# Four-layer gated cross-attention: mixed attention moved to a third lane with one PSUM bank, one bank of scores in the top-k lane beside it, two weight packs in one reloaded buffer

## What is computed

```python
x = x + tanh(g_xattn[0]) * performer(layernorm(x), ctx)          # causal linear attention, 16 heads of 8
x = x + tanh(g_ffn[0])   * (attention(layernorm(x)) + top2_linear_experts(layernorm(x)))
x = x + tanh(g_xattn[1]) * topk64_attention(layernorm(x), ctx)   # 8 heads of 64
x = x + tanh(g_ffn[1])   * gated_experts(layernorm(x))
x = x + tanh(g_xattn[2]) * attention(layernorm(x), ctx)          # 16 heads of 8
x = x + tanh(g_ffn[2])   * gelu_experts(layernorm(x))            # 8 experts and a shared one, 128 to 512 to 128
x = x + tanh(g_xattn[3]) * topk32_attention(layernorm(x), ctx)   # 16 heads of 8
x = x + tanh(g_ffn[3])   * mixed_attention(layernorm(x))
```

## Time and profile before

| what | value |
|---|---|
| median of three runs (lowest, highest) | 2736.93 us (2734.93, 2739.3) |
| the profiled execution, its own time | 2744.56 us |
| its span, first to last instruction | 2742.8 us |
| PE, DVE, ACT, POOL busy share of the span | 86%, 75%, 51%, 33% |
| blocks that hold MixedAttention beside other work | 3 x ORDER_3_0, 3 x ORDER_1_0, ORDER_LAST |

### The profile page before, as it was taken

The page is one execution under the profiler, slowest core; times in us unless marked ns, Lnnn a source line. Parts: engine busy times, 40 slices in busy tenths (PEclk is TensorE's granted clock), DMA queues, the critical chain, the costliest instruction groups (busy, mean ns, idle before and its releaser), DMA issues. The chain is left out here.

```text
span 2742.8 us, 41506 instructions
## 1 busy us (share of the span) xinstructions
PE 2347.1 (86%) x12585; PEld 1739.3 (63%) x12585; DVE 2063.7 (75%) x8036; ACT 1388.9 (51%) x3333; POOL 915.8 (33%) x1398
## 2 busy tenths in 40 slices
PE   5888888999889788899989878889998898889876
PEld 3555675676576567576657656657765665766655
DVE  1498969867696796958779589695878859698692
ACT  2444565644535356664543546566362355656441
POOL 4141214246244122424525221332542512142432
PEclk9889889899999889988999889998999898899997
DMA  5000000000000000000000000000000000000000
GB/s 227 7 1 1 1 1 1 1 7 3 7 3 1 2 1 1 1 1 7 3 7 3 1 2 1 1 1 7 3 1 6 3 1 1 1 1 1 1 1 4
DMA packets 9069, 22.14 MB, mean 8 GB/s; under 512 B 642, under 2 KB 7810, under 8 KB 8066
## 3 DMA queue, kind: packets, MB, share of 16 engines
q1 hardware_dynamic: 8834, 19.33, 1.9%
HBM read 18.28 MB, written 1.05 MB: 7 GB/s over the span
## 5 line engine op out<-in xcount | busy, mean ns | idle before, releaser
L182 DVE MATCH_REPLACE8 workQ<-top_eight,workQ 128x256 f32<-128x256 f32 x1664 | 692.6, 439 | 0.0
L184 DVE MAX8 top_eight<-workQ 128x8 f32<-128x256 f32 x1664 | 641.6, 441 | 0.3
L218 POOL TENSOR_TENSOR att_pQ<-att_pQ,top_rest 128x512 f32<-128x512 f32 x192 | 244.2, 1272 | 333.6 <-ACT top_rest L211 333.4
L719 PE MATMUL bank<-workP 128*128 128x256 f32 x1024 | 297.4, 417 | 35.2 <-ACT att_pP L849 24.4
L719 PEld LDWEIGHTS bank<-workP 128*128 128x128 f32 x1024 | 188.3, 203 | 111.7 <-issue 61.5
L849 ACT ACTIVATE att_pP<-bank,att_nmaxP 128x256 f32<-128x256 f32 x512 | 215.2, 476 | 76.0 <-DVE att_nmaxP L898 75.1
L898 DVE TENSOR_REDUCE att_nmaxP<-bank 128x2 f32<-128x512 f32 x256 | 178.3, 708 | 94.6 <-PE bank L719 94.0
L234 ACT ACTIVATE att_pTQ<-bank 128x512 f32<-128x512 f32 x192 | 115.3, 601 | 221.5 <-PE bank L112 221.1
L871 POOL TENSOR_SCALAR workP<-workP,const 128x256 f32<-128x256 f32 x256 | 122.2, 481 | 263.7 <-PE bank L719 207.3
L489 PE MATMUL bank<-workQ 128*128 128x256 f32 x512 | 153.2, 429 | 47.5 <-ACT att_pQ L201 37.6
L184 DVE MAX8 top_lead<-bank 128x8 f32<-128x256 f32 x384 | 150.3, 447 | 54.0 <-ACT top_rest L211 40.0
(11 more groups left out here) (289 smaller groups left out, 4917.0 us busy)
## 6 DMA issues: line engine op xcount, KB each, us to landing
pack3w<-in_pack3w SPq DMA_DIRECT2D x1, 4608.0 KB, 20.8
pack4w<-in_pack4w SPq DMA_DIRECT2D x1, 4096.0 KB, 31.0
pack<-in_pack SPq DMA_DIRECT2D x1, 2266.0 KB, 10.4
pack<-in_pack SPq DMA_DIRECT2D x1, 1028.0 KB, 7.3
mix_wb<-in_ctx SPq DMA_DIRECT2D x1, 1024.0 KB, 4.9
x_in<-in_x SPq DMA_DIRECT2D x8, 128.0 KB, 2.2
ctx_tok<-in_ctx SPq DMA_DIRECT2D x8, 128.0 KB, 2.2
ctxT<-in_ctxT SPq DMA_DIRECT2D x8, 128.0 KB, 2.4
```

The source lines that it names most:

```text
L182: ins = nc.vector.match_replace(self.work[:, u % 2, j, :], eight, src, GONE)
L184: ins = nc.vector.max(eight, src)
L218: self.k.nc.gpsimd.tensor_tensor(v, v, self.rest[:, :, :], ALU.subtract).then_inc(self.p_ready, 1)
L719: mm = self.k.nc.tensor.matmul(self.banks[u % 2][:, j * T:(j + 1) * T], self.q1[:, u % self.RING, j * P:(j + 1) * P], self.kT, start=True, ...
```

## The change

- MixedAttention leaves lane P and becomes a lane of its own, M (Chunk4), with bank 7 alone and its own buffers: `mix_z` (16 x 256 per partition), `mix_rest`, and a layernorm of its own. A block can hold Q, P and M.
- With one bank, the weights of two experts wait for the copy of the two before; q and k are added up in a first pass over the experts, then copied out, and v in a second pass, 8 steps more.
- Where M runs beside lane Q, lane Q has three banks, `narrow`: one for scores (bank 4), one for turning, one for its output. The scores of unit u + 1 then stand at round 2 of unit u (round 3 in Chunk1), in place of those of u + 2. In the other blocks it keeps four (`roomy`), in other roles: in Chunk1 q goes to banks 0 and 2 of the lane and waits for the copy of v.
- `pack3w` and `pack4w` share the buffer `expert_w`. `pack3w` is loaded at the start of each block ORDER_1_2, `pack4w` at the start of ORDER_3_0 and ORDER_LAST: eight loads in place of two.
- The waits and the swapped step that tied Performer to MixedAttention go; LinearExperts keeps its wait for the store of the old batch.
- All six order strings are new. ORDER_LAST has Q and M alone (M under the letter P).
- HeadAttention loses code that only the plain attentions used.

```diff
+        self.ring = 1 if self.banks[0] is self.banks[1] else 2
...
-        if u >= 2:
-            pe.wait_ge(self.exp_done, u - 1)
+        if u >= self.ring:
+            pe.wait_ge(self.exp_done, u - self.ring + 1)
...
-        u = self.at(s, 0, 3) + 2
-        if 2 <= u < H1:
+        u = self.at(s, 0, 3) + self.ring
+        if self.ring <= u < H1:
             self.score(pe, u)
```

```diff
-            if i >= 2:
-                pe.wait_ge(self.wb_ready, i - 1)
+            else:
+                pe.wait_ge(self.wb_ready, i)
...
-        i = self.at(s, 2, 0)
-        if i >= 0:
+        i = self.after_z(s)
+        if 0 <= i < self.PAIRS:
+            if i == 0:
+                pe.wait_ge(self.wb_ready, self.PAIRS)
+                if self.weights is not None:
+                    pe.wait_ge(self.weights, 16)
             pe.wait_ge(self.z_ready, i + 1)
...
+        if i >= self.PAIRS:
+            i -= self.PAIRS
+            if i == 0:
+                pe.wait_ge(self.qkv_copied, 2)
```

```diff
+        roomy, narrow = k.psum[4:8], [k.psum[4], k.psum[4], k.psum[5], k.psum[6]]
...
         with nc.Fori(0, NB // 2 - 1) as n:
             i = n * 2
-            run_block(k, [Chunk1(k, 1), Chunk2(k, 0)], ORDER_1_2)
-            run_block(k, [Chunk3(k, 0), Chunk2(k, 1)], ORDER_3_2)
-            run_block(k, [Chunk3(k, 1), Chunk0(k, 0, i, i + 2)], ORDER_3_0)
-            run_block(k, [Chunk1(k, 0), Chunk0(k, 1, i + 1, i + 3)], ORDER_1_0)
...
+            run_block(k, [Chunk1(k, 1, roomy), Chunk2(k, 0, True)], ORDER_1_2)
+            run_block(k, [Chunk3(k, 0, roomy), Chunk2(k, 1, False)], ORDER_3_2)
+            mix = Chunk4(k, 0, i, True)
+            run_block(k, [Chunk3(k, 1, narrow), Chunk0(k, 0, i + 2, mix.mix), mix], ORDER_3_0)
+            mix = Chunk4(k, 1, i + 1, False)
+            run_block(k, [Chunk1(k, 0, narrow), Chunk0(k, 1, i + 3, mix.mix), mix], ORDER_1_0)
```

More of the change, by code:

```diff
@@ L68, in cols @@
+    "PPPQQPQPPQQQQQQ")
 def cols(pack):
@@ L493, in projected @@
     def projected(self, s):
-        early = self.order[0:2] if self.order == "kvq" else ""
-        return early if s == 0 else self.order[len(early):] if s == 2 else ""
+        return "kv" if s == 0 else "q" if s == 2 else ""
     def project(self, pe, what):
@@ L514, in pe @@
             self.ln.pe(pe)
-        if s == 0 and self.before is not None:
-            self.before.wait_banks(pe)
         if s == 2:
@@ L1395, in pe @@
         if u >= 0:
+            if u == 0 and self.weights is not None:
+                pe.wait_ge(self.weights, 16)
             for c in range(FF2):
@@ L1504, in __init__, with after_z @@
         self.PAIRS = E16 // 2
-        self.units(6, self.PAIRS, 1, 2, self.SUM + self.PAIRS + 2)
+        self.units(6, self.PAIRS, 1, 1 + 2 * self.PAIRS, self.SUM + self.PAIRS + 2)
+    def after_z(self, s):
+        i = s - self.first - self.PAIRS - 1
+        return i if 0 <= i < 2 * self.PAIRS else -1
     def pe(self, pe, s):
-        nc, w, b = self.k.nc, self.k.w, self.banks
+        nc, w, b = self.k.nc, self.k.w, self.bank
         if s == 1:
@@ L1577, in act @@
     def act(self, act, s):
-        nc, b = self.k.nc, self.banks
+        nc, b = self.k.nc, self.bank
         if s == 1:
@@ L1722, with __init__ @@
 class Chunk0(Chunk):
[L1725 removed]
+    def __init__(self, k, lane, batch, old=None):
         self.k, self.batch, b = k, batch, k.psum[0:4]
[L1727 to L1733 removed]
@@ L1735, in steps @@
-    def steps(self):
-        steps = super().steps()
-        if len(self.stages) > 1 and self.mix is not None:
-            n = self.mix.steps
-            steps[n - 1], steps[n] = steps[n], steps[n - 1]
-        return steps
+        self.ctxT, self.load = k.ctxT[lane], k.sem("load")
+        att = PlainHeads(k, "P", 0, k.x_in, None, b, "b", router=("prob", "gate0", "bgate0"))
+        self.stages = [Performer(k, "P", k.x_in, self.ctxT, k.ctx_tok, b, self.load), att,
+                       LinearExperts(k, "P", k.x_in, k.x[lane], att, b, 4, old)]
@@ new lines, in sync, with __init__ @@
+        sp.dma_start(k.ctx_tok[:, :, :], k.ctx_dram[bass.ds(i * T, T), :].rearrange("(j p) d -> p j d", p=P)).then_inc(self.load, 16)
+        sp.dma_start(self.ctxT[:, :], k.ctxT_dram[:, bass.ds(i * T, T)]).then_inc(self.load, 16)
+class Chunk4(Chunk):
+    def __init__(self, k, lane, batch, load_weights):
+        self.k, self.weights = k, k.sem("pack4w_in") if load_weights else None
+        self.mix = MixedAttention(k, "M", k.x[lane], batch, k.psum[7], 7, self.weights)
+        self.stages = [self.mix]
+    def sync(self, sp):
+        if self.weights is not None:
+            w = self.k.pack_dram["pack4w"]
+            sp.dma_start(self.k.expert_w[:, 0:cols(PACK4W)], w).then_inc(self.weights, 16)
+        self.mix.sync(sp)
@@ L1840, in flamingo @@
                 at += n
+        k.expert_w = k.sb("expert_w", [P, max(cols(pack) for _, pack in TURNS)])
+        for name, pack in TURNS:
+            at = 0
+            for what, n in pack:
+                k.w[what] = k.expert_w[:, at:at + n]
+                at += n
+        k.pack_dram = {name: dram[name] for name, _ in TURNS}
         row = k.sb("rows", [1, cols(ROWS)])
```

297 lines of the change are left out of this document (124 added, 173 removed).

## The result

| | before | after |
|---|---|---|
| median (lowest, highest) | 2738.11 us (2734.93, 2740.07), 4 runs | 2614.25 us (2607.0, 2618.02), 4 runs |
| ratio, 95% interval | | 0.9545 [0.9531, 0.9558] |
| the profiled execution, its span | 2744.56, 2742.8 us | 2616.44, 2614.6 us |
| predicted | | 2679 us, 2625 to 2728 |

The account below looks back on a forecast made before the run. It took two chains waiting for each other's engines, no engine full, as the bound. Terms -20 - 47 + 4 + 4 + 1 = -58 from the profiled 2744.6, less 7.6 to the median, gave 2679 us, range 2625 to 2728.

Parts of the forecast that it names:

- What bounds the kernel: In ORDER_3_0 and ORDER_1_0: no engine full, two chains waiting for each other's engines, lane P's own length 165.9 of 173.1 us.
- MixedAttention beside lane P: Term for ORDER_3_0 and ORDER_1_0: with MixedAttention off lane P, engines' work sets the length; -20 and -47 us.
- I take two thirds of the way: In ORDER_3_0 and ORDER_1_0: two thirds of the possible gain, 6.8 and 15.8 us a block, three times each.
- the floors: Fullest engine's work plus 14.4 us for start, barrier and tail: 161.9 us for ORDER_3_0 (PE), 147.0 for ORDER_1_0 (DVE).
- Rival B: ORDER_3_0 and ORDER_1_0 gain their full 102 us, time 2640; needs PE and DVE over 90% full in ORDER_3_0; chance 0.14.
- New orders elsewhere: Blocks FIRST, 1_2 and 3_2 keep their work, only orders change: 0, bounded by 15 us either way over nine blocks.
- One bank for lane M: Last block +4 us (between 0 and 8), 0.99 us a pair of experts; no cost in the other six blocks.
- One bank of scores: Lane Q: +4 us in ORDER_LAST, where a late score shows at once; no cost in ORDER_1_0.
- Rival C: Single bank of scores stalls DVE in ORDER_3_0 and ORDER_LAST: 99 us, time 2774; score wait over 30 us; chance 0.10.
- q of Chunk1: q waits for v's copy: hidden in ORDER_1_0, at most 0.60 us in eight blocks with Chunk1, +1 us in all.
- the reloads: Eight weight loads, first read over 40 us into their blocks: nothing, or 31 - 20 us once if met early.
- wrong at the root: Sign against the prediction: blocks of 3_0 and 1_0 above 170 us, or a gain coming from 1_2 and 3_2.

Follow-up runs that it names:

- e4: The kernel before without lane Q in the loop's blocks ORDER_3_0 and ORDER_1_0, lane P alone there: 2634.6 us, blocks 153.2 and 153.5.
- e5: The changed kernel without lane M in the loop's blocks ORDER_3_0 and ORDER_1_0: 2553.3 us, blocks 148.0 and 137.9.
- e1: The changed kernel with the old order strings for ORDER_FIRST, ORDER_1_2 and ORDER_3_2 alone: 2638.7 us, ratio 0.9634.
- e2: The kernel before with the new order strings for ORDER_FIRST, ORDER_1_2 and ORDER_3_2 alone: 2714.0 us, ratio 0.9922.
- e9: The changed kernel without lane M in ORDER_3_0 and ORDER_1_0, lane Q given back its second bank of scores there: 2558.0 us, ratio 0.9334.
- e15: The changed kernel with seven more weight loads, in ORDER_3_2 and in M of ORDER_1_0: 2615.3 us, ratio 0.9543.
- e12: The changed kernel run again with nothing altered: 2616.7 us, ratio 0.9542 to the kernel before.
- e10: The changed kernel with ORDER_3_2 made of the new string's first 70 letters and the old one's last 80: 2630.7 us, ratio 0.9600.

## Why the prediction was wrong

- **What bounds the kernel: right in kind.** It said that two chains wait for each other's engines and no engine is full. e4 measured lane P alone at 153, not 166, so the lanes held each other up by more than it thought.
- **MixedAttention beside lane P: the size failed.** The step that failed is "I take two thirds of the way", with its reason that with PE and DVE both nearly full the floors would not be reached. They were: 160.5 against 161.9, 145.8 against 147.0, so 35 and 75 us in place of 20 and 47. Rival B, at 0.14, was this case, though not by the condition it was given: DVE did not have to be over 90% full in ORDER_3_0, it was 81%, and PE 94%. For ORDER_1_0 the floor stood on DVE and its overhead came out near (145.8 - 131.0 = 14.8, against the 14.4 taken), but it is no constant: without M it was 137.9 - 119.7 = 18.2, and with a lower clock 149.0 - 131.0 = 18.0. For ORDER_3_0 the floor stood on PE. As a rule for a block it fails (e5: 148.0 us for 125 to 130); that its number was near may be luck or not, the runs don't tell. A part of both gains is the clock, for which the sum had no term; how large a part is not measured.
- **New orders elsewhere: failed.** "I take 0", bounded by 15. They brought 25 (e1, e2). The bound came from one block's change of 3 us between passes. It left out PE's clock: a shift of one or two steps in a string can go with a stretch at 1.2 GHz, and with it the length of a block changes by 5 us.
- **One bank for lane M: the sign right, the price mis-sized.** +6.3 in place of +4 in the last block, since a pair took 1.30 us and not 0.99. That it costs nothing in the covered blocks is borne out in ORDER_LAST and not tested in the other six; in series it was 4.6 to 12.8 (the prediction had 8).
- **One bank of scores.** In place of +4 ORDER_LAST grew by 1.3 us, less than it varies between runs. Rival C did not happen: 14.9 us of waits, under its 30. That they stand in place of others is shown without M alone (e9). In series the bank is worth 9 to 15 us a block.
- **q of Chunk1, the reloads: right** as far as the runs can tell; e15 shows the reloads at nothing.
- **The sum.** By block -35 - 75 - 25 - 4 + 1 + 6 = -132, with 2.2 us more in Chunk0 alone, 0.5 in ORDER_FIRST and the rest rounding: 2744.6 less 128 is the profiled 2616.4. Two terms, 43 and 29 us, are more than the whole miss of 65 in the median. The prediction had named a gain from 1_2 and 3_2 as "wrong at the root", and 29 of the 128 us are that.

## What to carry to other kernels

Where two lanes wait for each other and no engine is full, a third lane can bring the block all the way to the fullest engine's work plus the block's start and tail, as the lengths of both blocks had it here; do not put that case at the far end. What a single buffer costs is a question of the order: price it uncovered (here 5 to 15 us a block), then ask whether other lanes' steps stand in its gaps. And never price a changed issue order at zero: read the granted clock in short pieces, and look for the stretches where it falls, since here a few steps moved went with 5 us a block.

## What the hardware showed that was not expected

The same block of instructions has two lengths in one execution, 145.8 at a mean clock of 0.98 and 149.0 at 0.96 (e12), 162.2 and 165.8 (e10), and nearly all of the difference is one stretch of two pieces, in which PE runs in part at 1.2 GHz. A block that no edit touches can switch between its lengths: ORDER_3_2 of the kernel before took 165.3 us in the first pass, and 159.9 in that of e4, whose instructions are the same up to there. Idle work that holds the clock up pays where it stands in nobody's way and costs where it does: in the last block 2.3 us won behind the scores, 1.7 lost ahead of them, with a clock of 0.91 in place of 0.77.
